# A decoder layer on one core: the transposes of the self attention's probabilities in two parts, with other products between

## The reference, cut to what matters

```python
scores = jnp.einsum('bkgtd,bksd->bkgts', Qg, K) * scale
scores = jnp.where(causal, scores, jnp.finfo(scores.dtype).min)
attn = jax.nn.softmax(scores, axis=-1)
out = jnp.einsum('bkgts,bksd->bkgtd', attn, V)
...
return out @ Wp.T
...
x = x + _L0_attn_ref(_layernorm(x, axis=-1), ...)
x = x + _L0_xattn_ref(_layernorm(x, axis=-1), ctx_512, ...)
```

## Time and profile before

| what | value |
|---|---|
| time, median of 3 executions | 561.45 us (560.05 to 563.21) |
| profiled execution: its own time / its span | 559.17 us / 557.3 us |
| mean granted TensorE clock over the span | 0.998 |
| PE busy | 526.8 us, 95% of the span |
| DVE, ACT, POOL busy | 400.8, 302.4, 282.6 us |
| rounds 1 to 3 and the last two batches | about 55 to 180 us of the span |

### The profile page before, as it was taken

One profiled execution on the slowest core, in us unless ns is written; L12 is line 12 of the kernel. 1 busy time (PEld: TensorE's weight loads), 2 busy tenths in 40 slices (PEclk: granted clock), 3 DMA queues, 4 the chain that ended last, 5 costly groups with the idle time before them and its releaser, 6 DMA issues. The chain is left out here.

```text
span 557.3 us, 9714 instructions
## 1 busy us (share of the span) xinstructions
PE 526.8 (95%) x3440; PEld 374.2 (67%) x3443; DVE 400.8 (72%) x909; ACT 302.4 (54%) x693; POOL 282.6 (51%) x360
## 2 busy tenths in 40 slices
PE   4989999999989999999999999999999999999995
PEld 4667776767767666576666776677678766885442
DVE  5675797797586698866877467894576667786863
ACT  3164735635655677655776356775466653621430
POOL 0579643464715776812666215693154552572660
PEclk9999999999999999999999999999999999999999
DMA  8976745766451630243693333244030019125928
GB/s 248 271 266 219 229 140 155 272 188 203 173 172 52 170 132 2 38 97 112 177 279 86 80 95 84 42 77 76 0 115 8 1 34 420 35 81 111 211 96 263
DMA packets 46242, 76.77 MB, mean 138 GB/s; under 512 B 20082, under 2 KB 30100, under 8 KB 45300
## 3 DMA queue, kind: packets, MB, share of 16 engines
q1 hardware_dynamic: 42948, 63.60, 37.0%
q0 software_dynamic: 2224, 10.73, 8.8%
q10 hardware_dynamic: 1024, 1.84, 1.0%
HBM read 57.36 MB, written 28.23 MB: 154 GB/s over the span
## 5 line engine op out<-in xcount | busy, mean ns | idle before, releaser
L2133 POOL TENSOR_TENSOR xprob<-xprob,erec 128x375 f32<-128x375 f32 x112 | 93.9, 843 | 129.1 <-DVE erec L1751 128.8
L1340 ACT ACTIVATE xprob<-s_ps,nmax 128x375 f32<-128x375 f32 x112 | 64.0, 572 | 55.2 <-DVE nmax L1746 53.1
L1746 DVE TENSOR_REDUCE nmax<-s_ps 128x1 f32<-128x375 f32 x112 | 59.3, 536 | 0.0
L2126 POOL TENSOR_TENSOR prob<-prob,rec 112x1792 f32<-112x1792 f32 x8 | 25.5, 3184 | 51.5 <-DVE rec L1654 51.3
L62 PE MATMUL s_ps<-kvt,qt_hl 128*128 128x376 f32 x112 | 48.1, 429 | 2.0 <-ACT xprob L1340 1.3
L1729 DVE SCALAR_TENSOR_TENSOR pt_hl<-f_ps,pt_hl 125x384 f16<-125x384 f32 (+1 forms) x62 | 38.0, 613 | 13.7 <-ACT pt_hl L1318 12.6
L62 PE MATMUL k_ps<-ow,ctx_hl 128*128 128x512 f16 (+1 forms) x104 | 39.6, 381 | 0.0
L64 PE MATMUL k_ps<-ow,ctx_hl 128*128 128x512 f16 (+1 forms) x104 | 39.4, 379 | 0.0
L63 PE MATMUL k_ps<-ow,ctx_hl 128*128 128x512 f16 (+1 forms) x104 | 39.4, 379 | 0.0
L63 PE MATMUL s_ps<-kvt,qt_hl 128*128 128x376 f32 x112 | 37.4, 334 | 0.0
L64 PE MATMUL s_ps<-kvt,qt_hl 128*128 128x376 f32 x112 | 37.4, 334 | 0.0
(11 more groups left out here) (380 smaller groups left out, 1494.4 us busy)
## 6 DMA issues: line engine op xcount, KB each, us to landing
w<-w_dram SPq DMA_DIRECT2D x6, 1024.0 KB, 10.0
raw_b<-in_raw SPq DMA_DIRECT2D x8, 640.0 KB, 5.2
raw_m<-in_raw SPq DMA_DIRECT2D x8, 576.0 KB, 4.7
raw_q<-in_raw SPq DMA_DIRECT2D x8, 512.0 KB, 6.9
ow_dram<-bw_sb SPq DMA_DIRECT2D x8, 512.0 KB, 5.5
ow_raw<-ow_dram SPq DMA_DIRECT2D x8, 512.0 KB, 3.3
qw_raw<-aw_dram SPq DMA_DIRECT2D x16, 256.0 KB, 3.1
w_dram<-in_w POOLq DMA_DIRECT2D x8, 512.0 KB, 5.7
```

Of the source, the lines that this page charges most:

```text
L1340: act.activation(xprob[z][:, 0:L], s_bank(n, k)[:, 0:L], ACT.Exp, bias=nmax[:, z:z + 1], accum_out=esum[:, z:z + 1]).then_inc(xexp_done, 1)
L1746: dve.tensor_reduce(nmax[:, z:z + 1], s_bank(n, k)[:, 0:L], X, ALU.max, negate=True).then_inc(xmax_done, 1)
L2126: pool.tensor_tensor(prob[q][:, :, :, :], prob[q][:, :, :, :], rec[q][:, :, :].unsqueeze(3).broadcast_to([T, PER, GROUPS, T]), ALU.mult).t ...
L2133: pool.tensor_tensor(xprob[z][:, 0:L], xprob[z][:, 0:L], erec[:, z:z + 1].broadcast_to([128, L]), ALU.mult).then_inc(xp_ready, 1)
```

## The change

- `turn_probs` and `copy_probs` take a list of j; the four turns stand in two parts, (0, 1) and (2, 3).
- Rounds 1 to 3, q = 0: the second `out_weight` matmul stands between the parts; `query_weight` stands ahead of `apply_probs`, behind it before.
- Rounds 1 to 3, q = 1: the mask matmuls are a function of their own; those of j = 3, 2 stand between the parts, those of j = 1, 0 behind them.
- The last two batches: half of a `query_pair` stands between the parts and half behind; in the other one `query_heads(0, 1)` stands between the parts, and `x_scores(0, 0)` ahead of `apply_probs`.
- On ACT the copies of q = 0 in rounds 1 to 3 are parted by the copy of the first `out_weight`, and the copy of `at_sb` stands ahead of `heads_high`.

DVE, POOL and SP keep their order.

```diff
@@ PE, rounds
-                    turn_probs(i, 0)
+                    turn_probs(i, 0, (0, 1))
                 out_weight(p, 1)
                 if i:
-                    apply_probs(i, 0)
+                    turn_probs(i, 0, (2, 3))
...
                 query_weight(p)
+                if i:
+                    apply_probs(i, 0)
                 turn_context(p)
...
-                    turn_probs(i, 1)
+                    turn_probs(i, 1, (0, 1))
+                masks(i, 0, (3, 2))
+                if i:
+                    turn_probs(i, 1, (2, 3))
+                masks(i, 0, (1, 0))
                 scores(i, 0)
@@ PE, the last two batches
-            turn_probs(ROUNDS, 0)
-            query_pair(0, 1)
+            turn_probs(ROUNDS, 0, (0, 1))
+            query_pair(0, 1, (0, 1))
+            turn_probs(ROUNDS, 0, (2, 3))
+            query_pair(0, 1, (2, 3))
...
-            turn_probs(ROUNDS, 1)
+            turn_probs(ROUNDS, 1, (0, 1))
             query_heads(0, 1)
+            turn_probs(ROUNDS, 1, (2, 3))
+            x_scores(0, 0)
             apply_probs(ROUNDS, 1)
-            x_scores(0, 0)
@@ ACT, rounds
-                    copy_probs(i, 0)
+                    copy_probs(i, 0, (0, 1))
                 copy_out_weight(p, 0)
+                if i:
+                    copy_probs(i, 0, (2, 3))
                 context_squares(p)
                 copy_out_weight(p, 1)
+                copy_query_weight(p)
                 if i:
                     heads_high(i, 0)
-                copy_query_weight(p)
```

More of the change, by code:

```diff
@@ L812, in turn_qk, with masks @@
                     turn(f_ps[bank], src, qkt_done)
-            def scores(i, q):
+            def masks(i, q, js):
                 b = 2 * i + q
-                pe.wait_ge(b_copied, 2 * b + 2)
+                if js[0] == PER - 1:
+                    pe.wait_ge(b_copied, 2 * b + 2)
                 if b == 0:
                     pe.wait_ge(setup, 2)
-                for j in reversed(range(PER)):
+                for j in js:
                     if j == 1:
@@ L825, in scores @@
                               start=True, stop=False, skip_group_check=True)
+            def scores(i, q):
+                b = 2 * i + q
                 pe.wait_ge(qkt_copied, 2 * b + 2)
@@ L832, in scores, with turn_probs @@
                 mm.then_inc(s_done, 1)
-            def turn_probs(i, q):
+            def turn_probs(i, q, js):
                 c = 2 * (i - 1) + q
[L837 to L840, removed]
+                if js[0] == 0:
+                    pe.wait_ge(p_ready, c + 1)
+                    if q == 0:
+                        wait(pe, x2_low, c)
+                for j in js:
                     if q == 1 and j == 1:
@@ L903, in x_take, with query_pair @@
                 return bank_of(n, name)
-            def query_pair(n, i):
+            def query_pair(n, i, ks=range(KC)):
                 u = n // HALF
[L907 to L910, removed]
+                if ks[0] == 0:
+                    if n == 0 and i == 0:
+                        pe.wait_ge(qkt_copied, 2 * B)
+                    pe.wait_ge(qw_low, qw_count(u, i))
+                    x_take(n, f"Q{i}")
+                bank = bank_of(n, f"Q{i}")
                 tok = slice((u // OCTS) * HT, (u // OCTS + 1) * HT)
-                for k in range(KC):
+                for k in ks:
                     mm = mm3(pe, bank[:, 0:HT], (qw[:, i, 0, k * 128:(k + 1) * 128], qw[:, i, 1, k * 128:(k + 1) * 128]),
                              (xn2_hl[:, 0, k, tok], xn2_hl[:, 1, k, tok]), start=(k == 0), stop=(k == KC - 1))
-                mm.then_inc(filled, 1)
+                if ks[-1] == KC - 1:
+                    mm.then_inc(filled, 1)
             def query_heads(n, i):
@@ L1185, in _ @@
                 turn_query_weight(p + 1)
+                masks(i, 1, (3, 2, 1, 0))
                 scores(i, 1)
-            turn_probs(ROUNDS, 0)
-            query_pair(0, 1)
+            turn_probs(ROUNDS, 0, (0, 1))
+            query_pair(0, 1, (0, 1))
+            turn_probs(ROUNDS, 0, (2, 3))
+            query_pair(0, 1, (2, 3))
             sum_squares()
@@ L1238, in exp, with copy_probs @@
                 act.activation(prob[q][:, :, :, :], prob[q][:, :, :, :], ACT.Exp, scale=SCALE).then_inc(s_exp, 1)
-            def copy_probs(i, q):
+            def copy_probs(i, q, js=range(PER)):
                 c = 2 * (i - 1) + q
-                wait(act, pv_done, c)
-                for j in range(PER):
+                if js[0] == 0:
+                    wait(act, pv_done, c)
+                for j in js:
                     act.wait_ge(pt_done, 4 * c + j + 1)
```

## The result

The changed kernel takes 563.13 us (median of 20 executions, 560.67 to 566.55) against 561.40 us for the kernel before (20 executions of the same comparison): ratio 1.0043, 95% interval 1.0023 to 1.0063, or 2.4 us slower (1.3 to 3.5). The ratio on record is not the quotient of the two medians; these lie 1.73 us apart, or 0.31%, which is inside the interval. A second comparison, on another occasion, gave 1.0036 (1.0017 to 1.0055). The forecast was 562.9 us. The profiled execution of the changed kernel took 563.92 us, with a span of 562.1 us.

A forecast was written before the change was run, and what follows sets the result against it. PE was taken to set the pace, with DVE close behind. Rounds 1 and 2 lose 0.8 us each, round 3 0.2, the last two batches gain 0.3: +1.5 us on the median 561.45, so 562.9 us; 8-in-10 range 560.4 to 564.8.

The forecast's parts named there:

- The gaps: Turns of rounds 1 to 3: PE loses 0.35 us at q = 0, 0.36 at q = 1; closing them gains 2.1 us gross.
- The wait for m_sb: Turn of q = 0, rounds 1 to 3: the query product, now earlier, waits about 0.8 us for DVE's m_sb.
- The value products and what hangs on them: Rounds 1 and 2: value products end at 99.1, not 97.59; heads' cast 1.45 us later, norm ends 1.0 to 1.1 later.
- aw_sb and the masks: Rounds 1 and 2: aw_sb comes late, so the mask of j = 0 starts 0.8 us later; a mask waits about 0.5 us.
- The last two batches: End of self attention: first turn's saving is waited away; after the second turn the next query product starts 0.3 us earlier.
- All that follows is pulled along by PE: Last two batches: everything behind the earlier query product moves with it, so its 0.3 us gain is kept.
- The sign that the prediction named: At the end, project_out's wait for the heads' low part should grow by some 0.4 us.
- The gain arrives: Rival: m_sb stands in time and PE does not wait at q = 0; 2.4 us faster, 559.0 us; chance 0.09.
- The norm collides worse: Rival: both norm instructions of rounds 1 and 2 take 1.49 us beside POOL; +3.5 us, 565.0 us; chance 0.13.
- Nothing left: Rival: gaps partly modelled transpose spacing, never PE's, and the m_sb wait is filled; sum near 0, about 561.4 us; chance 0.1.

The follow-up runs named there:

- a3: Changed kernel with two VectorE moves: m_sb copy ahead of q = 1's rotary work, next round's layer norm behind the aw_sb copy; ratio 0.9985 to the kernel before.
- d: Changed kernel with both VectorE moves of a3, but the last two batches left as before; ratio 0.9954 to the kernel before.
- f1: Changed kernel with both VectorE moves of a3, and lent_scales moved some 8 us later; ratio 0.9955 to the kernel before.
- c1: Changed kernel with the turn of q = 0 whole again and its value products ahead of the query product; ratio 0.9987 to the kernel before.
- g2: c1 with both VectorE moves of a3; ratio 0.9998 to the kernel before.
- a2: Changed kernel with the next round's layer norm behind the aw_sb copy on VectorE in rounds 1 and 2; ratio 1.0036 to the kernel before.
- a1: Changed kernel with the m_sb copy ahead of q = 1's rotary work on VectorE in rounds 1 to 3; ratio 0.9979 to the kernel before.
- b1: Kernel before with both VectorE moves of a3 and nothing of the change; ratio 0.9991 to the kernel before.
- c2: Kernel before with the change of the last two batches alone, rounds as before; ratio 1.0003 to the kernel before.

## Why the prediction was right, and where not

The forecast was +1.5 us as 0.8 + 0.8 + 0.2 - 0.3; the traces show 0.80 + 0.76 + 0.22 + 0.24 = +2.0. The three rounds are right in size and in mechanism; the last term has the wrong sign. That 562.9 us lies so near 563.13 us is in part luck, since this term alone is 0.54 us off.

- **The gaps.** The `probt` waits of the rounds are gone, as forecast. Their worth was put at 0.71 us a round; with nothing else binding (a3, d, f1) it is 0.9 us. The turn of q = 1 gives 0.38 us (round 3 of c1, 9.50 - 9.12), as forecast (0.36). That of q = 0 gives 0.55 us (g2 and a3, 9.12 - 8.57), not 0.35, for two of its terms were too dear: the first eight transposes take 0.77 us (95.48 to 96.25) where 0.87 was taken from the second eight, and the fold behind them takes 0.87 us (96.25 to 97.12) where 0.96 was taken. The second eight take 0.87 us without a stall too (102.89 to 103.76 in a2); why the halves differ stays open.
- **The wait for m_sb.** Forecast: three, some 0.8 us each. Measured: three, 1.1 us each. `m_sb` is done 98.99 - 95.48 = 3.51 us behind the turn, exactly as in the earlier trace rows; PE merely comes earlier: it is ready 2.5 us behind the turn (a1, where it does not wait: 99.09 - 96.59), not 2.70. What counts, the start of the product, was forecast at 97.2 - 93.63 = 3.57 us behind the turn and is at 99.14 - 95.48 = 3.66. a1 shows the mechanism: when that copy stands six rotary instructions earlier, the wait goes and round 3 gains 1.15 us.
- **The value products and what hangs on them.** The context's transposes start 5.57 us behind the turn (forecast 5.47, before 4.97). The norm takes 2.00 us, as forecast (about 2.1; before 2.55), and ends at 104.30, again 0.29 us behind the GpSimd instruction that stands beside it (102.83 + 1.18 = 104.01). In a2, where the norm starts later, the pair takes 1.41 us, and ends at 103.89, 0.29 us behind a GpSimd instruction that ends at 103.60.
- **aw_sb and the masks.** A wait of 0.5 us was forecast, and the profile prints 0.20 us. The rest is in the mask of j = 1, which starts at 104.80, right behind `kvt_hl` (104.21 + 0.54 = 104.75), without a bracket. Together they are what round 3, which has no norm, is shorter: 10.25 - 9.72 = 0.53 us. a2 takes the norm out of the way and gives 9.72 us in all three rounds, so it is the norm in VectorE's queue. (The forecast's own ends of the norm, 102.4 to 102.6 against 101.48, make it 0.9 to 1.1 us later, not 1.0 to 1.1; the sum does not hang on it.)
- **The last two batches: the step that failed.** The query product of the last pair starts 0.33 us earlier, as forecast (0.3). The sentence "All that follows is pulled along by PE" is wrong. The pair itself gives 0.10 us back: its first three matmuls, which now stand behind the value products and not behind the first scores, take 182.39 - 181.67 = 0.72 us, before 179.76 - 179.16 = 0.60, and so `project_out` starts 2.54 us behind that product, before 2.44. The sign that the prediction named, a wait of `project_out` for `ot_hl` longer by 0.4 us, did not come: this last `project_out` waits in neither profile, and the listed wait (0.5 us before, 0.6 now) is that of the first of the two batches, whose 0.1 us is lost again in the second turn's wait for GpSimd (it starts 13.55 us behind the scores, before 13.58). The last query heads lose another 0.47 us, by `lent_scales` beside GpSimd. Both are shown by distances in the trace, and the second by f1. The prediction had followed ACT and VectorE only up to the value products; what VectorE queues behind them, and what GpSimd runs then, was not read.
- **The rivals.** "The gain arrives" fell, since `m_sb` is late; a3, d and f1 show that the gain is there once it is not. "The norm collides worse" fell: the pair takes 2.00 us, not 3.0. "Nothing left" fell: the gaps were PE's, 0.9 us a round.

Three totals lie above their stages: a2, a3 and g2 measured some 1.0, 1.6 and 0.8 us above what their stages say. For a2 and g2 that is within the intervals. In a3, 8 of 12 runs had a mean granted clock of 0.994 or less (5 of 35 in the kernel before beside it); d and f1, with the same rounds, had 2 and 1 of 12 and came out as their stages say. The runs on record settle most of it: among those at 0.997 and above the median span of a3 is 555.5 us (3 runs) against 558.3 us (17), and among those at 0.994 and below it is 558.25 us (8 runs) against 561.2 us (5). At a like clock a3 is thus 2.8 and 2.95 us faster, where its stages say 2.4; its total is diluted by its share of runs at the low clock. These groups are small: for b1, in whose stages nothing moved, the same comparison at 0.997 and above gives -1.3 us. Why a3 had so many such runs stays open.

## What to carry to other kernels

When an instruction is moved ahead of another in a queue that is always busy, look up when its operand arrives, even where the profile shows no wait: a slack of 0.45 us that no list of waits shows decided this change, and two moves on another engine turned its loss in the rounds into a gain of 2.7 us. In all, -0.5% was measured with a third move (f1) or with the last two batches left as they were (d); the two moves alone (a3) measured 0.9985 (0.9963 to 1.0008). Then follow the moved work until it meets the next fixed point, on every engine whose queue it shifts; the gain of the last step here was lost for the most part to two instructions on 128x8 elements. A move that is worth nothing in the old kernel (b1) can be what makes a change pay.

## What the runs showed of the hardware

**Two small VectorE instructions were held for as long as GpSimd's instruction ran.** Operations of 0.22 and 0.23 us (f1) took 0.80 and 2.05 us when they started behind a GpSimd instruction, and ended 0.02 to 0.03 us after it; started ahead of GpSimd's, as in the kernel before, the second took 0.23 us. Here the rule of the Trainium skill ("SBUF — State Buffer", Who interferes with whom) agrees: when a VectorE instruction in a two-port mode and a GpSimd instruction meet, the first to come holds the shared pair of ports for its whole instruction and the other blocks; in which mode these two ran no run shows. The prediction reckoned by that rule that a whole layer norm instruction of 0.54 us follows GpSimd's, and so 0.5 us less in the sum. That did not come: in all 12 profiles each of the four norm instructions of rounds 1 and 2 ended 0.28 to 0.29 us behind the end of a GpSimd instruction, though one takes 0.54 us where no GpSimd instruction stands beside it. Part of its time thus lies ahead of that end; which part, no run shows.

**The granted clock falls for some 7 us in the experts' stage, in some executions, with the rounds changed or not (c2).** PE from 484 to 494 us in the changed kernel's profile (length, busy us and instructions, granted clock, DMA share, GB/s):

```profile
482.00:484.00 2.00, 2.00 (x19) 1.00 0.00 0
484.00:486.00 2.00, 2.00 (x16) 0.80 0.01 4
486.00:488.00 2.00, 2.00 (x10) 0.50 0.38 119
488.00:490.00 2.00, 2.00 (x10) 0.50 0.20 64
490.00:492.00 2.00, 2.00 (x7) 0.50 0.39 122
492.00:494.00 2.00, 2.00 (x17) 0.99 0.30 91
```

0.50 is 1.2 GHz, 1.00 is 2.4 GHz. In the rows just before the fall, and while the clock rose again, PE was busy throughout. It stands in 5 of the 12 profiles (both of the changed kernel, a3, c2, d), where the experts' stage takes 23.3 to 23.4 us, and is absent from the other 7, with 21.2 us: some 2.2 us. The instructions there are the same in all; what sets it off stays open. A profile with the fall must not be compared by its span with one without it.
